# A transformer layer of two cross-attention blocks in one loop: the same operations issued in another order

## The chip, the cores and the metric

The kernel runs on one core of one Trainium2 chip. The metric is the device time of one execution in microseconds. A core has five engines that each take their own instructions in order: TensorE (PE in the profile; PEld is its weight load), VectorE (DVE), ScalarE (ACT), GpSimd (POOL) and SyncE (SP), which here only issues DMAs. They meet at semaphores.

## The reference

64 samples of 128 rows by 320 columns, `x`, and a context of 128 rows by 192 columns, `ctx`, go through two blocks. The first attends from `x` to the first 124 rows of the context (8 heads), adds a second result from the last four context rows ("tokens"), projects, and adds `x`. The second is a transformer layer: self attention (20 heads), cross attention to the context (20 heads), and a gated feed-forward, each after a layer norm and with a residual.

```python
query = hidden_states @ Wq; keyt = enc @ Wk; valt = enc @ Wv
hs = _mha(query, keyt, valt)
ca_hs1 = _mha(ca_q1, residual, residual)          # token queries attend to x
ca_hs2 = _mha(ca_hs1 @ Wq, ca @ Wk_ca, ca @ Wv_ca)
x = (hs + ca_hs2) @ Wout + b_out + residual
h1 = _ln(x, n1_g, n1_b)
x = _attn(h1, h1, q1, k1, v1, o1_w, o1_b, heads) + x
h2 = _ln(x, n2_g, n2_b)
x = _attn(h2, context, q2, k2, v2, o2_w, o2_b, heads) + x
h3 = _ln(x, n3_g, n3_b)
a, g = jnp.split(h3 @ ff_w1 + ff_b1, 2, axis=-1)
ff = a * jax.nn.gelu(g, approximate=False) @ ff_w2 + ff_b2
return ff + x
```

## The kernel before

Two samples make a step (`G = 2`, 32 steps). The loop runs 33 passes, and one pass holds work of several steps at once: the first block of step i, self attention and cross attention of the step before it, and the feed-forward of the one before that. A head that computes factors and loads weights stands ahead of the loop, and a last feed-forward behind it.

The order of the work is written out by hand. `BODY` names the "jobs" of a pass, the results that PE writes to six PSUM banks in turn (`J_BANKS`); each engine's own program then calls its part of every job in its own order. A job may start when the reader of the job six places ahead has released the bank (`bank_free`). Names used below:

- `XTj_b`: transpose of the normalised rows of block b for layer j. ScalarE writes the high half precision part of it to `hTn` (`high_blocks`), VectorE the low part (`low_blocks`).
- `K1T0..2`, `Q1T0..2`: chunks of self keys and queries from `hTn`. ScalarE writes the high part (`high_shifted`), VectorE the whole value (`whole_shifted`), GpSimd the difference (`low_split`). `Q0Tk`, `K0Tk` (first block), `K2Tk` (cross keys): chunks whose low part VectorE writes (`low_chunk`). SP writes the chunks to scratch memory in DRAM (`put`, L360) and reads them back stacked by head as `Qs`, `Ks`, `Q0s`, `K0s` (`stack`, L364).
- `S0..S27`: scores of a unit of four heads; VectorE takes the row maxima (`maxima`, L896). `mx0..mx7`: those maxima transposed, into `mxs`.
- `T0..T27`: the same scores the other way round, less the maxima. ScalarE writes two exponentials of each, `P` and `PT` (`exps`, L649 and L650), and GpSimd their difference (`low_probabilities`, L462). `attend(n)` then multiplies `PT` with the values (V0, VX, V1, V2). Units 0 to 3 are the token queries, 4 to 13 self, 14 to 23 cross, 24 to 27 the first block.
- `outTj_b`, `outMj_b`: transpose and projection of the attention output, then `residual`, `deviation` (GpSimd) and `norm`. `ff0..ff9`, `y0`, `y1`: feed-forward. `kca`, `vca`, `M4`, `caT`, `s4`, `p4T`, `hs`: the tokens' path. `G`: the token gains for the next pass.

SP's queue matters too. `load_step(i + 1, i)` issues the nine loads of the next step (`xT`, `cT`, `ca32`, `xin`, and `cT2`, this step's context once more, for the cross keys and values that the next pass uses), each of which adds 16 to `step_loaded`. It stands behind the stacks of the first block and behind a wait for the low part of `V0_1`, the last reader of `cT`:

```python
                sp.wait_ge(v_done, v_job(i, LOOP_JOBS, "V0_1"))
                sp.wait_ge(xa_ready, i * G + G)
                sp.wait_ge(ca_ready, i + 1)
                sp.wait_ge(vx_ready, i * G + G)
                load_step(i + 1, i)
```

## Time and profile before

| | |
|---|---|
| median of 3 runs | 4520.15 us (4511.48 to 4526.72) |
| the profiled execution | 4524.91 us |
| its span | 4523.1 us |
| PE busy | 3916.9 us, 87% |
| DVE, ACT, POOL busy | 57%, 50%, 44% |
| TensorE clock granted, mean | 0.90 of full speed |
| bytes moved by DMA | 232.60 MB, 51 GB/s |

A row of a timeline gives the start in us from the span's start, the duration, the engine, the source line, the operation, what is written and read, how many instructions the row merges, and in square brackets the idle time before it with what ended it. TensorE's clock has two levels, 2.4 GHz (1.0) and 1.2 GHz (0.5); a granted clock between them is the mean of a stretch. In the list of waits a row says who waited at which line for whose result, the total, the count and the longest.

### The profile page before, as it was taken

The numbers are of one execution on the slowest core, as the hardware profiler recorded it, in microseconds if no ns is written. First come the engines' busy times: TensorE is split into PE (matmuls) and PEld (weight loads), VectorE is DVE, ScalarE is ACT, GpSimd is POOL, SyncE is SP. The second block draws the span as 40 slices with busy tenths as digits, with TensorE's granted clock in tenths as the row PEclk, the third lists the DMA queues.
The fourth block names the chain that finished last, engine by engine and source line by source line (L and its number), as shares of the span: only waits on it lengthen the run. The fifth ranks groups of instructions, "written<-read, shape, count | busy, mean of one in ns | idle before, by whom it ended". The sixth has DMA issues, their size and how long they took to land.

```text
span 4523.1 us, 114162 instructions
## 1 busy us (share of the span) xinstructions
PE 3916.9 (87%) x39220; PEld 3138.1 (69%) x39220; DVE 2589.3 (57%) x6409; ACT 2246.6 (50%) x3834; POOL 1978.1 (44%) x2297
## 2 busy tenths in 40 slices
...
GB/s 125 55 53 48 35 51 45 56 58 52 54 35 51 46 56 58 51 54 32 47 52 56 58 49 57 32 47 52 56 58 49 57 32 47 52 56 57 49 47 28
DMA packets 394133, 232.60 MB, mean 51 GB/s; under 512 B 24806, under 2 KB 393054, under 8 KB 393182
## 3 DMA queue, kind: packets, MB, share of 16 engines
...
## 4 chain that ended last, share of the span: by engine, by line
PE 34%; issue 30%; POOL 24%; DVE 7%; ACT 2%; DMA 2%; POOLq 1%; DVEq 0%; SPq 0%; ACTq 0%
PE bank L1291 31%; POOL PT L462 11%; POOL ca_heads L495 3%; PE bank L1332 2%; POOL cK L469 1%; POOL cQ L469 1%; DMA out<-X 1%; POOL XA L455 1%; POOL VX L484 1%; DVE OB L944 1%; POOL VX L483 1%; DVE OB L966 1%; POOL OA L482 1%; ACT P L631 1%; POOL XB L455 1%
## 5 line engine op out<-in xcount | busy, mean ns | idle before, releaser
L462 POOL TENSOR_TENSOR PT<-P,PT 128x512 f16<-128x512 f32 (+1 forms) x924 | 1066.8, 1155 | 1073.5 <-ACT PT L650 1073.5
L896 DVE TENSOR_REDUCE mx<-bank 128x4 f32<-128x512 f32 (+1 forms) x924 | 598.8, 680 | 236.9 <-PE bank L1291 232.1
L1291 PE MATMUL bank<-hT,w_ff_w 128*128 128x256 f16 x5440 | 645.7, 275 | 0.8 <-DVE hT L925 0.8
L1291 PE MATMUL bank<-mxs,pick 84*128 84x128 f16 (+1 forms) x3696 | 613.0, 242 | 0.0
L1291 PEld LDWEIGHTS bank<-hT,w_ff_w 128*128 128x128 f16 x5440 | 539.0, 100 | 73.1 <-DVE hT L925 1.2
L1291 PE MATMUL bank<-V,PT 128*128 128x17 f16 (+1 forms) x9504 | 371.3, 175 | 117.9 <-POOL PT L462 114.0
L1291 PEld LDWEIGHTS bank<-V,PT 128*128 128x128 f16 (+1 forms) x9504 | 334.0, 100 | 177.1 <-POOL PT L462 163.6
L1291 PE MATMUL bank<-Qs,Ks 96*128 96x128 f16 x2640 | 452.3, 248 | 2.4
L1291 PEld LDWEIGHTS bank<-mxs,pick 84*128 84x128 f16 (+1 forms) x3696 | 418.7, 115 | 26.1 <-issue 11.3
L631 ACT ACTIVATE P<-bank,ff_b,scale 128x256 f32<-128x256 f32 x340 | 191.6, 564 | 411.6 <-PE bank L1291 336.3
L1291 PE MATMUL bank<-w_ff,F 128*128 128x320 f32 x1360 | 389.9, 434 | 1.3 <-DVE F L972 1.3
L502 POOL TENSOR_TENSOR rstd<-mv,eps 128x1 f32<-128x1 f32 x198 | 41.1, 208 | 659.6 <-DVE mv L960 658.3
L972 DVE SCALAR_TENSOR_TENSOR F<-bank,ff_b,P 128x256 f32<-128x256 f32 x340 | 163.8, 482 | 280.7 <-ACT P L631 279.7
L1291 PE MATMUL bank<-hTn,w_k 128*128 128x256 f16 (+1 forms) x792 | 160.6, 387 | 180.5 <-DVE hTn L925 180.5
L1291 PEld LDWEIGHTS bank<-Qs,Ks 96*128 96x128 f16 x2640 | 298.9, 114 | 19.4 <-DVE mxs L905 5.4
L1291 PEld LDWEIGHTS bank<-w_ff,F 128*128 128x128 f32 x1360 | 248.9, 190 | 89.7 <-DVE F L972 1.5
L649 ACT ACTIVATE P<-bank,log_p,out_factor 128x512 f32<-128x512 f32 x330 | 256.1, 776 | 51.1 <-PE bank L1291 31.7
L790 DVE TENSOR_SCALAR whole<-bank,factor,qk_b 128x256 f32<-128x256 f32 (+1 forms) x297 | 157.0, 538 | 205.4 <-ACT cK L581 145.2
L649 ACT ACTIVATE P<-bank,log_p,exp_self 128x512 f32<-128x512 f32 x330 | 256.8, 778 | 27.5 <-PE bank L1291 24.9
L1291 PEld LDWEIGHTS bank<-hTn,w_k 128*128 128x128 f16 (+1 forms) x792 | 105.9, 141 | 233.9 <-DVE hTn L925 188.3
L650 ACT ACTIVATE PT<-bank,log_p,exp_self 128x512 f16<-128x512 f32 x330 | 256.6, 777 | 0.0
L650 ACT ACTIVATE PT<-bank,log_p,out_factor 128x512 f16<-128x512 f32 x330 | 253.8, 769 | 0.0
...
## 6 DMA issues: line engine op xcount, KB each, us to landing
...
xin<-in_x SPq DMA_DIRECT2D x34, 320.0 KB, 3.4
```

What stands on the lines that cost most here:

```text
L455: nc.gpsimd.tensor_tensor(dst[:, b, :], src[:, b, :], bias[:, j, :], ALU.add).then_inc(ready, 1)
L462: nc.gpsimd.tensor_tensor(PT[0:keys, n % PT_SLOTS, 1, :], P[0:keys, n % P_SLOTS, :], PT[0:keys, n % PT_SLOTS, 0, :], ALU.subtract).then_in ...
L469: nc.gpsimd.tensor_tensor(dst[0:r, 1, k, :], whole[0:r, m % 3, :], dst[0:r, 0, k, :], ALU.subtract)\
L495: nc.gpsimd.tensor_tensor(ca_heads[:, :, :], ca16[:, :].unsqueeze(1).to_broadcast([rows, HEADS0, GS]), mask_ca[:, :].unsqueeze(2).to_broad ...
L631: nc.scalar.activation(gate[:, t % 2, :], bank[:, 0:GS], ACT.Gelu, scale=scale[:, 1:2], bias=ff_b[:, FFT + t:FFT + t + 1]).then_inc(a_done, 1)
L649: nc.scalar.activation(P[0:keys, n % P_SLOTS, :], bank[0:keys, :], ACT.Exp, bias=log_p[0:keys, :], scale=by)
L650: nc.scalar.activation(PT[0:keys, n % PT_SLOTS, 0, :], bank[0:keys, :], ACT.Exp, bias=log_p[0:keys, :], scale=by).then_inc(a_done, 1)
L790: nc.vector.tensor_scalar(whole[0:r, m % 3, :], bank[0:r, 0:GS], factor[0:r, FQ2:FQ2 + 1], qk_b[0:r, c + k:c + k + 1], ALU.mult, ALU.add). ...
L896: nc.vector.tensor_reduce(mx[:, g % 2, 4 * u:4 * u + 4], bank[:, :].rearrange("p (h s) -> p h s", h=4)[:, :, 0:keys], axis=AX.X, op=ALU.ma ...
L972: nc.vector.scalar_tensor_tensor(out=F[:, t, :], in0=bank[:, GS:2 * GS], scalar=ff_b[:, t:t + 1], in1=gate[:, t % 2, :], op0=ALU.add, op1= ...
L1291: return nc.tensor.matmul(o, lhsT, rhs, start=start, stop=stop)
L1332: last = nc.tensor.transpose(bank[0:r, k * S:(k + 1) * S], src[:, b, at[k]:at[k] + r], ident[:, :])
```

## The change

`BODY`, and with it the programs of PE, ACT and DVE, are put in another order; the operations stay. In short:

- A pass begins with XT0_0, the first queries Q0T0 and Q0T1, the token scores S0 and S1, XT0_1, Q0T2, S2, S3, and only then K1T. Before, the two transposes came first and K1T directly behind them.
- The value product of unit n stands behind the exponents of unit n + 2 (before: n + 1).
- K0T0, K0T1 and the transposes caT stand ahead of S4. K2T0 and K2T1 move from behind the feed-forward to between the self exponents, with a wait for `step_loaded` ahead of K2T0; K2T2 and the V2 products move in among the cross exponents; the products of y0 and y1 are cut into more pieces and moved forward.
- VectorE's `turn_factors` runs at the end of a pass for the next, not at its start.
- SP writes Q0T first, on semaphores of its own (`q0_put`, `k0_put` for `first_put`), and `load_step` issues the two `cT2` loads first.
- The column of ones of V0 and V2 is written once per block.

```diff
 BODY = jobs_of("""
-    XT0_0 XT0_1 K1T0 K1T1 K1T2 Q1T0 Q1T1 Q1T2
+    XT0_0 Q0T0 Q0T1 S0 S1 XT0_1 Q0T2 S2 S3 K1T0 mx0 K1T1 K1T2 Q1T0 mx1 Q1T1 Q1T2
...
             def load_step(i, before):
+                for k, r in enumerate(CHC):
+                    sp.dma_start(cT2[0:r, k, :], d["cT"][before, k * r:(k + 1) * r, :]).then_inc(step_loaded, 16)
                 for k, r in enumerate(CH0):
...
             def one_pass(i, stores):
+                put_lows(i, "Q0T", cQ, CH0, s_q0, AT0, q0_put)
                 put_splits(i, "K1T", cK, s_k1, self_put)
...
-                put_lows(i, "Q0T", cQ, CH0, s_q0, AT0, first_put, self_stacked)
-                put_lows(i, "K0T", cK, CH0, s_k0, AT0, first_put)
+                put_lows(i, "K0T", cK, CH0, s_k0, AT0, k0_put, self_stacked)
                 sp.wait_ge(j_full, done(i - 1, LOOP_JOBS.number("T27"), "J"))
-                sp.wait_ge(first_put, i * STACK_STORES + STACK_STORES)
+                sp.wait_ge(q0_put, i * CROSS_STORES + CROSS_STORES)
                 stack(Q0s, s_q0, D0, Q_PARTS, first_stacked)
+                sp.wait_ge(k0_put, i * CROSS_STORES + CROSS_STORES)
                 stack(K0s, s_k0, D0, K_PARTS, first_stacked)
...
             def turn_factors(i):
-                dve.wait_ge(next_ready, i + 1)
+                dve.wait_ge(next_ready, i + 2)
...
+                pe.wait_ge(step_loaded, i * LOADS_STEP + 2 * LOADS_STEP)
+                chunk(i, "K2T", 0, "k2", CHC, cT2, AT1, CH1)
+                attend(i, 7)
                 exponents(i, 9)
-                attend(i, 7)
+                chunk(i, "K2T", 1, "k2", CHC, cT2, AT1, CH1)
+                attend(i, 8)
                 exponents(i, 10)
-                attend(i, 8)
+                attend(i, 9)
...
                 ff(i, L, 0)
                 attend(i, 12)
+                ff(i, L, 1)
                 attend(i, 13)
-                ff(i, L, 1)
+                ff(i, L, 2)
                 turn_out(i, 1, 1)
...
-                bank = j_ahead(i, "y0", 2)
-                v_job_done(i, L, "ff8")
-                ff_products(bank, 0, 0, 6)
+                bank = j_ahead(i, "y0", 5)
+                v_job_done(i, L, "ff7")
+                ff_products(bank, 0, 0, 5)
                 scores(i, 14)
                 scores(i, 15)
```

First place: PE at the start of a pass. In the kernel before, the two transposes of XT0 (`OA`) and then the chunks of K1T (`w_k`):

```order
L1298 ISA
L1332 MATMUL bank<-ident,OA 128x128 x3
L1501 REGISTER_ALU
L1298 REGISTER_ALU
L1332 MATMUL bank<-ident,OA 128x128 x3
L1336 ISA
L1298 REGISTER_ALU
L1291 MATMUL bank<-hTn,w_k 128x256 x8
```

And in the changed kernel, where `w_Wq` is a chunk of Q0T and `G,ca_heads` a unit of token scores:

```order
L1342 MATMUL bank<-ident,OA 128x128 x3
L1308 REGISTER_ALU
L1301 MATMUL bank<-xT,w_Wq 120x256 x3
L1308 REGISTER_ALU
L1301 MATMUL bank<-xT,w_Wq 120x256 x3
L1430 REGISTER_ALU
L1346 REGISTER_ALU
L1301 MATMUL bank<-G,ca_heads 128x128 x4
L1308 REGISTER_ALU
L1301 MATMUL bank<-G,ca_heads 128x128 x4
L1511 REGISTER_ALU
L1308 REGISTER_ALU
```

The second transpose comes behind two query chunks and two units of scores; one more chunk and two more units follow it ahead of `w_k`.

Second place: DVE at the start of a pass. Before, behind the loop's branch, the factors (L880 to L888) and the low parts of XT0 (`hTn`):

```order
L1154 ISA
L880 COPY out_factor<-factor 128x2
L772 ISA
L881 COPY out_factor<-next_factor 128x1
L882 COPY factor<-next_factor 128x12
L772 REGISTER_ALU
L883 TENSOR_SCALAR out_inverse<-out_factor 128x3
L772 REGISTER_ALU
L886 TENSOR_SCALAR out_inverse<-out_inverse,scale 128x3
```

Now, with `cQ` the low part of a query chunk and `mx` the maxima of a unit:

```order
L1164 ISA
L930 SCALAR_TENSOR_TENSOR hTn<-bank,hTn 128x2x128
L933 SCALAR_TENSOR_TENSOR hTn<-bank,hTn 64x128
L787 REGISTER_ALU
L803 SCALAR_TENSOR_TENSOR cQ<-bank,factor,cQ 120x256
L787 REGISTER_ALU
L803 SCALAR_TENSOR_TENSOR cQ<-bank,factor,cQ 120x256
L789 ISA
L904 TENSOR_REDUCE mx<-bank 128x4
```

The factors are gone from here; two query chunks and two units of maxima stand between the low parts of XT0_0 and XT0_1.

Third place: PE in the self attention of the changed kernel, behind T8 (`Qs,Ks` and `mxs,pick`); the ISA row at L1656 is the new wait for `step_loaded`, and `cT,w_k` is K2T0:

```order
L1301 MATMUL bank<-Qs,Ks 128x128
L1301 MATMUL bank<-mxs,pick 128x128
L1656 ISA
L1308 REGISTER_ALU
L1301 MATMUL bank<-cT,w_k 128x256 x2
L1478 REGISTER_ALU
L1301 MATMUL bank<-V,PT 128x17 x12
L1346 REGISTER_ALU
```

In the kernel before this chunk stands behind the feed-forward, with no wait for the loads of its own ahead of it.

## Rows read from the trace of the kernel before

**Rows 1.** The page, part 1: busy time, share and instructions of each engine.
```profile
PE 3916.9 (87%) x39220; PEld 3138.1 (69%) x39220; DVE 2589.3 (57%) x6409; ACT 2246.6 (50%) x3834; POOL 1978.1 (44%) x2297
```
**Rows 2.** The waits of PE: engine, line, waited for, total, times, longest.
```profile
PE bank L1291 <- DVE hTn L925: 186.7, 66, 5.9
PE bank L1291 <- POOL PT L462: 151.0, 232, 1.5
...
PE bank L1332 <- DVE OB L944: 70.8, 99, 1.3
...
PE bank L1291 <- DMA Qs<-scratch_q: 7.3, 17, 0.6
```
**Rows 3.** Line L1519, once a pass: duration, first and last start.
```profile
L1519 PE MATMUL bank<-ident,p x33: 272/273/273, 179.4 to 4424.3; 128*128 128x128 f32 x33
```
**Rows 4.** Windows of one pass: length, busy PE, PEld, DVE, ACT, POOL, clock, DMA share, GB/s.
```profile
2360.90:2379.90 19.00, 13.03 (x68) 8.69 (x67) 12.19 (x36) 4.12 (x9) 4.89 (x8) 0.91 0.05 15
2379.90:2402.10 22.20, 19.84 (x203) 15.40 (x204) 10.19 (x28) 10.81 (x19) 9.85 (x12) 0.92 0.53 76
2402.10:2427.00 24.90, 22.50 (x279) 18.33 (x280) 16.32 (x36) 17.68 (x31) 11.31 (x11) 0.95 0.44 111
2427.00:2463.00 36.00, 33.72 (x287) 27.41 (x286) 22.03 (x56) 12.17 (x21) 15.89 (x22) 0.99 0.27 45
2463.00:2490.80 27.80, 23.89 (x346) 20.55 (x345) 14.91 (x35) 22.43 (x36) 17.62 (x18) 0.82 0.03 10
```
**Rows 5.** Timeline of PE around the start of that pass and at S4.
```profile
2373.34 0.87 PE L1332 MATMUL bank<-ident,OA 128*128 128x128 f32 x6
2379.88 4.58 PE L1291 MATMUL bank<-hTn,w_k 128*128 128x256 f16 x24 [5.67 <-DVE hTn L925]
2384.40 2.91 PE L1291 MATMUL bank<-hTn,w_q 128*128 128x256 f16 x24
...
2402.07 0.62 PE L1291 MATMUL bank<-Ks,Qs 96*128 96x128 f16 x8 [0.37 <-DMA Qs<-scratch_q]
```
**Rows 6.** Timeline of DVE: last residual, first instruction behind the branch, token maxima.
```profile
2368.62 0.55 DVE L955 SCALAR_TENSOR_TENSOR XA<-bank,out_inverse,XA 128x320 f32<-128x320 f32 x1 [1.54 <-PE bank L1291]
...
2376.96 0.36 DVE L880 COPY out_factor<-factor 128x2 f32<-128x2 f32 x1 [2.46 <-issue]
...
2388.49 1.27 DVE L896 TENSOR_REDUCE mx<-bank 128x4 f32<-128x512 f32 x2
```
**Rows 7.** Timeline of POOL: the last split of Q1T.
```profile
2388.65 0.66 POOL L469 TENSOR_TENSOR cQ<-whole,cQ 64x256 f16<-64x256 f32 x1 [0.31 <-DVE whole L790]
```
**Rows 8.** Timeline of DVE: the low part of V0_1.
```profile
2419.90 0.54 DVE L809 SCALAR_TENSOR_TENSOR V<-bank,factor,V 128x320 f16<-128x320 f32 x1
```
**Rows 9.** Timeline of SP's queue: first and last loads of a step, stack of cross queries.
```profile
2420.89 1.38 SPq L351 DMA_DIRECT2D xT<-in_xT  x3
...
2424.44 0.82 SPq L357 DMA_DIRECT2D cT<-in_cT  x2
...
2449.54 1.34 SPq L364 DMA_DIRECT2D Qs<-scratch_q  x3
```
**Rows 10.** The DMA view: issues, KB each, median us to landing.
```profile
xin<-in_x SPq DMA_DIRECT2D x34, 320.0 KB, 3.4
```
**Rows 11.** Timeline of ACT in the cross units: P of units 15, 16, 19 and 20.
```profile
2465.20 0.78 ACT L649 ACTIVATE P<-bank,log_p,out_factor 128x512 f32<-128x512 f32 x1
...
2466.57 0.78 ACT L649 ACTIVATE P<-bank,log_p,out_factor 128x512 f32<-128x512 f32 x1
...
2471.02 0.78 ACT L649 ACTIVATE P<-bank,log_p,out_factor 128x512 f32<-128x512 f32 x1 [0.20 <-PE bank L1291]
...
2472.61 0.78 ACT L649 ACTIVATE P<-bank,log_p,out_factor 128x512 f32<-128x512 f32 x1
```
**Rows 12.** The page, part 5: group of L462, GpSimd's difference.
```profile
L462 POOL TENSOR_TENSOR PT<-P,PT 128x512 f16<-128x512 f32 (+1 forms) x924 | 1066.8, 1155 | 1073.5 <-ACT PT L650 1073.5
```
**Rows 13.** Line L357, the loads of cT2: time to landing.
```profile
DMA to landing us min/median/max: 2.8/4.4/8.5
```
**Rows 14.** Timeline of PE: the transpose behind Q2T, and S14 with S15.
```profile
2445.46 0.33 PE L1530 MATMUL bank<-ident,ext_wide 128*128 128x128 f32 x1
...
2456.30 0.61 PE L1291 MATMUL bank<-Ks,Qs 96*128 96x128 f16 x8
```

More of the change, by code:

```diff
@@ L109 @@
 BODY = jobs_of("""
[L110 to L118 removed]
+    XT0_0 Q0T0 Q0T1 S0 S1 XT0_1 Q0T2 S2 S3 K1T0 mx0 K1T1 K1T2 Q1T0 mx1 Q1T1 Q1T2
+    T0 V1_0 T1 kca T2 V1_1 T3 vca M4 K0T0 K0T1 caT0 caT1
+    S4 S5 S6 K0T2 S7 S8 V0_0 mx2 S9 S10
+    T4 S11 T5 S12 V0_1 T6 S13 s4 T7 mx3 T8 K2T0 T9 K2T1 T10 T11 outT1_0 T12 outM1_0 T13
+    ff0 ff1 ff2 outT1_1 ff3 outM1_1 ff4 p4T ff5 XT1_0 XT1_1 ff6 Q2T0 Q2T1 Q2T2 mT ff7 mB ff8 ff9
+    S14 S15 S16 S17 S18 y0 mx4 S19 S20
+    T14 S21 T15 K2T2 T16 S22 T17 S23 T18 mx5 T19 S24 T20 S25 T21 mx6 T22 outT2_0 T23 S26 V2_0
+    T24 outM2_0 T25 S27 mx7 V2_1 T26 outT2_1 T27 outM2_1 hs0 outT0_0 hs1 y1 outM0_0 outT0_1 XT2_0 XT2_1 outM0_1 G
 """)
@@ L355, in load_step @@
                 sp.dma_start(xin[:, :, :], d["x"][i, :, :, :].rearrange("g s c -> s g c")).then_inc(step_loaded, 16)
-                for k, r in enumerate(CHC):
-                    sp.dma_start(cT2[0:r, k, :], d["cT"][before, k * r:(k + 1) * r, :]).then_inc(step_loaded, 16)
             def put(src, k, r, dst, at, landed):
@@ L1149, in _ @@
             link(-1, nc.vector.tensor_scalar(exp_self[:, :], exp_self[:, :], D1 ** -0.5, None, ALU.mult))
[L1150 removed]
+            for b in range(G):
+                ones_column(V1, b, HEADS1, D1, out_factor[:, 1:2])
+            turn_factors(-1)
             low_tokens(-1, HEAD_JOBS)
@@ L1694, in _ @@
                 scores(i, 20)
-                chunk(i, "K2T", 1, "k2", CHC, cT2, AT1, CH1)
                 exponents(i, 14)
```

363 lines of the change are left out of this document (182 added, 181 removed).

## The prediction

> **What bounds the kernel now.** I read the page's busy line first: PE is busy for 87% of the span and no other engine for over 57% [rows 1]. So the time is PE's work, at the clock that it is granted, plus PE's idle time. The list of waits, kept to PE, says what ends that idle time: 187 us for `hTn` from DVE, 151 us for `PT` from POOL, 71 us for `OB` from DVE, 7 us for a DMA of Qs [rows 2]. One transpose that occurs once a pass starts at 179.4 us and, 32 passes later, at 4424.3 us [rows 3]: a pass takes 132.6 us, and there are 33.
>
> I then took one pass apart in five stretches by the windows view [rows 4], with these marks: end of the value product of unit 27; start of the first key chunk K1T0; start of S4, the first self scores; start of ff0; start of T14, the first cross exponents; end of unit 27 again. They last 19.0, 22.2, 24.9, 36.0 and 27.8 us: 129.9 us, a quick pass. The clock column matters as much: 0.82 in the fifth stretch, 0.91 and 0.92 in the first two. The mean pass is 2.7 us longer than this one, with the same instructions; I put that down to more half clock in some passes.
>
> **The change, stretch by stretch.** No instruction's shape changes but that the column of ones is now written per block (some 0.3 us of DVE a pass, beside other work). What is priced is where waits fall.
>
> *Stretch 1, unit 27 to K1T0: 19.0 becomes about 18.0 us.* Before, PE ends its two transposes and idles 5.67 us until K1T0 [rows 5]. The DVE rows show why: after the token gains (`G`) DVE stands 2.46 us at the loop's branch, ended by "issue", and only then come the factors (1.3 us) and the low parts of XT0 (1.5 us), which take it to K1T0 [rows 6]. The change puts Q0T (three chunks, some 1.35 us each) and S0 to S3 (0.9 us) in that hole, and the factors ahead of the branch. But the hole is DVE's chain, not a lack of PE work, and the chain gets other links. After the change it runs: last residual with its statistics 1.35, factors 1.3, norm 0.45, tokens 0.5, branch 2.46, low XT0_0 0.75, two low query chunks 0.95, two maxima 1.27 (the pair of [rows 6]), low XT0_1 0.7: 9.7 us. Against that, the old chain from the residual's start at 2368.62 to K1T0 at 2379.88 is 11.3 us [rows 5, 6]. The last residual itself starts later, since low parts and norms of the block before now stand ahead of it on DVE: 8.3 us behind unit 27 instead of 7.7. Sum 18.0. PE idles still, in three pieces of 2.1, 2.3 and 1.3 us, because Q0T2 reuses the bank that the low part of XT0_0 must release.
>
> *Stretch 2, K1T0 to S4: 22.2 becomes 20.6 us.* S4 starts when the stacked queries have landed; PE waited 0.37 us for that DMA [rows 5]. The chain is: K and Q chunks on PE, last split on POOL, ending at 2389.31 [rows 7], then puts and stacks until 2402.07, which is 12.8 us. At full clock, with the two maxima's transposes put in, the chunks take 5.9 us (24 matmuls 2.9 us; the K group took 4.58, mostly at half clock [rows 5]). Then 1.9 to the last split, and 12.8. PE's own work there: 19.8 us busy [rows 4], less 1.7 for K's half clock, 1.4 and 0.9 for Q0T0 and S0 to S3, and 2.6 more for K0T and two transposes, some 18.4 us. So it waits about 2 us for the DMA, a wait that takes the place of the old one and hides as much half clock in the slow passes.
>
> *Stretch 3, S4 to ff0: 24.9 becomes 27.7 us, the dear one.* PE now waits for `step_loaded` ahead of K2T0, and the count is that of all nine loads of the next step. SP can issue them only when the low part of V0_1 is done: it ended at 2420.44, and the first load was issued at 2420.89 [rows 8, 9]. The nine issues take 4.4 us and the `xin` load lands 3.4 us after its issue [rows 9, 10]. That cT2 is now issued first helps nothing. V0_1's low part comes 9.6 us behind S4 (it was 18.4): 5.1 us to T4 (five maxima at 0.65 and what is between), two units of ScalarE at 1.37 us [rows 11], two copies. So the loads are complete at 9.6 + 0.45 + 4.4 + 3.4 = 17.8 us. PE comes to K2T0 at 12.0 us (two more units on ScalarE, then POOL's 1.155 us [rows 12]) and stands 5.8 us. Behind it in PE's queue are all of units 7 to 13, so ScalarE and POOL run dry too. Then five units, two chunks, one projection: 9.9 us. Bounds: no stall if the loads are earlier than I think (22.3 us), and 31 us if the last load lands 3 us later, which is within the range of landings of the cT2 loads [rows 13].
>
> *Stretch 4, ff0 to T14: 36.0 becomes 34.1 us.* Out go K2T0 and K2T1 (about 0.9 us each, now in stretch 3), and one of the waits for `OB` shrinks by some 0.5 us, since ff1 and ff2 stand ahead of the transpose. But one ff block less, and one product of y0 less, stand between Q2T and S14. Q2T ended as the transpose behind it began, at 2445.46; the stacked queries were issued from 2449.54, and S14 started at 2456.30 without a wait [rows 9, 14]. So they land at most 10.8 us behind Q2T; I take 10.3. PE gets there after 7.3: a new wait of 3 us. 19.3 + 10.3 + 4.5 = 34.1.
>
> *Stretch 5, T14 to unit 27: 27.8 becomes 25.7 us.* This is where the value products lag. ScalarE paces it: a unit each 1.37 us, 1.59 us where PE is at half clock [rows 11]. The lag takes away PE's waits for `PT`, but those are the shadow of ScalarE's pace: 14 x 1.36 + 3.3 for the copies that now lie inside (two of V2, K2T2, two of hTn, three maxima) = 22.3, and 3.4 for the first exponent, POOL, and what PE has queued before unit 27.
>
> Sum at full clock: 18.0 + 20.6 + 27.7 + 34.1 + 25.7 = 126.1 us against 129.9.
>
> **The clock** takes most of that back. The old pass went to half clock after its 5.67 us of idleness (K group 4.58 instead of 2.9 us) [rows 5], and in the light work of stretch 5, at 0.82 [rows 4]. The new one has idle pieces of 5.7 us together ahead of K1T0, 2.5 ahead of S4, 5.8 ahead of K2T0, 3 ahead of S14. I add 1.7 for K1T, 1.2 for K2T and its neighbours, 1.0 for stretch 5: 3.9, so a pass of 130.0, and 130.3 with what slow passes still lose. Bounds: 0 and 8 us.
> The Trainium skill, page "TensorE: Matmul & The Clock Gate", section "HAM oscillation — how this bites in real kernels", says that a DMA wait in front of each short burst of matmuls throttles the engine each time, so that every burst starts cold; by it the three DMA waits of the new pass would each be paid for twice. The K group here agrees for one idle stretch; no row shows it yet for a DMA wait.
>
> Mean pass 132.6 to 130.3: 2.3 us x 33 = 76 us. Head and tail do not change but for one factors chain (1.3 us). The profiled execution took 4524.9 us; less 76 is 4449. It stood 5 us above the median of 4520, so I say **4445**.
>
> **Rivals.**
> - *The K2T stall is not there, or short* (the loads are early enough, or PE is late). For: the sum brings PE to K2T0 with no clock loss on the way, and a PE that comes late waits less. Then stretch 3 is 22.3 to 24, a pass 125 to 127: 4270 to 4340. Against: the nine loads follow V0_1 strictly [rows 8, 9], and they move with it. Chance 0.22.
> - *Slower, by the K2T stall*: one wait at `step_loaded`, 9 us rather than 5.8, with ScalarE and POOL empty behind it. It decides from about 8 us: 2.3 us of net gain are used up. At 9 us a pass is 133.5, so 4555. For: it stands in PE's in-order queue in the middle of a stage paced by ScalarE. Chance 0.15.
> - *Slower, by the clock*: each new wait is followed by a half-clock stretch as K1T's is, and the units between T9 and ff0, light work as in stretch 5, stay there too. 4 us more than I added: 134.3 a pass, 4580. This is the rule cited above. Chance 0.08.
> - *No difference*: gains and stalls cancel, 4507 to 4534. Chance 0.08.
> - *The forecast's case*, 4340 to 4505: 0.47.
>
> **Numbers.** Faster 0.22 + 0.47 = 0.69, same 0.08, slower 0.23. "Same" is within 0.3%, about what a measurement of this kernel can tell. The range is 4290 to 4565: it leaves out some 0.08 below and 0.10 above.
>
> **What would show it.** In PE's waits, `hTn` from DVE falls from 187 to below 120 us, but does not vanish; `PT` falls below 60; a wait for a DMA of `xin` or `cT` appears at the first K2T chunk, near 190 us in all; waits for Qs grow from 7 to over 100 us. The DVE keeps its 2.4 us at the branch. If the wait at K2T0 is below 2 us a pass, the third stretch is wrong and the time is near 4300; if S4 does not wait for its DMA, stretch 1 or PE's load is mis-sized; if K1T runs at full clock and the total clock rises above 0.93, the clock term is.

## The result, and the profile after

The changed kernel took 5074.9 us (median of 4 runs, 5068.3 to 5077.5) against 4523.2 us for the kernel before (4 runs): a ratio of 1.122, 95% interval 1.120 to 1.125. It is 12% slower. The forecast was 4445 us, 1.7% faster, with a range to 4565: wrong in sign and far outside the range. The ratios of the experiments below are each against the kernel before as timed in the same round (medians 4514.8 to 4531.4 us).

The page's busy line of the changed kernel answers to [rows 1], and the list of waits, PE only (who waited at which line, for whom: us in total, times, longest), to [rows 2]:

```profile
PE 4233.4 (84%) x39220; PEld 3361.7 (66%) x39220; DVE 2543.2 (50%) x6482; ACT 2246.4 (44%) x3834; POOL 1977.4 (39%) x2297
```
```profile
PE bank L1301 <- DMA Qs<-scratch_q: 148.8, 64, 3.4
PE bank L1301 <- DVE hTn L933: 123.8, 105, 1.7
PE bank L1301 <- DMA xin<-in_x: 110.8, 33, 5.1
PE bank L1301 <- DVE mxs L913: 78.0, 99, 1.5
PE bank L1301 <- POOL PT L463: 77.7, 142, 1.0
PE bank L1342 <- DVE OB L952: 53.4, 33, 2.0
PE bank L1342 <- issue: 49.3, 32, 1.9
PE bank L1301 <- issue: 48.7, 32, 1.7
```

PE's busy time grew by 316 us with the same matmuls, which is 9.6 us a pass; its idle time grew by 227 us, 6.9 a pass. So the waits alone do not tell the story: the larger part is that the same matmuls took longer. The windows view of one pass, with the marks of [rows 4], shows where it went (columns: window, length, busy PE, PEld, DVE, ACT, POOL with counts, granted clock, DMA share, GB/s):

```profile
2341.17:2362.69 21.52, 17.19 (x92) 12.22 (x87) 13.74 (x38) 4.57 (x10) 4.86 (x8) 0.84 0.08 22
2362.69:2383.95 21.26, 17.96 (x197) 14.73 (x195) 11.34 (x34) 11.06 (x21) 10.26 (x12) 1.00 0.57 82
2383.95:2418.89 34.94, 30.21 (x262) 24.49 (x263) 13.01 (x30) 16.05 (x27) 10.37 (x9) 0.52 0.27 72
2418.89:2454.94 36.05, 32.22 (x280) 25.82 (x279) 20.59 (x54) 13.03 (x22) 16.43 (x22) 0.99 0.25 38
2454.94:2491.19 36.25, 29.62 (x359) 23.46 (x360) 15.49 (x37) 22.58 (x36) 17.63 (x18) 0.81 0.05 15
```

Read the third row first: S4 to ff0 ran at a clock of 0.52, half clock almost without a break, and took 34.9 us instead of 24.9 [rows 4]. The fifth, T14 to unit 27, took 36.3 instead of 27.8 us at about the old clock. Those two hold the loss. The second stretch had full clock (0.92 before).

For the experiments I use means over the passes of one traced execution (29 passes, worked out from PE's rows and the recorded clock). The mark at the end of unit 27 is the start of the PE instruction behind its value product; in e7 PE stands idle for a microsecond there, and the mark is the product's end. Each cell is length in us, then half-clock time.

| kernel, median us | unit 27 to K1T0 | to S4 | to ff0 | to T14 | to unit 27 | pass |
|---|---|---|---|---|---|---|
| before, 4523 | 19.1 / 2.8 | 23.6 / 7.0 | 25.4 / 4.3 | 36.0 / 0.7 | 28.2 / 11.5 | 132.3 / 26.3 |
| after, 5075 | 20.8 / 5.4 | 21.1 / 0.1 | 35.0 / 32.3 | 36.1 / 0.5 | 36.3 / 14.0 | 149.2 / 52.2 |
| e1, 5015 | 20.7 / 5.4 | 23.2 / 0 | 31.6 / 18.7 | 34.8 / 0.9 | 37.5 / 17.8 | 147.7 / 42.7 |
| e16, 4929 | 20.4 / 4.8 | 21.1 / 0 | 30.6 / 10.2 | 35.1 / 1.5 | 37.8 / 18.7 | 145.1 / 35.2 |
| e3, 4933 | 21.0 / 5.9 | 21.0 / 0.1 | 30.7 / 27.2 | 36.0 / 0.8 | 36.5 / 14.0 | 145.1 / 48.0 |
| e5, 4825 | 21.0 / 5.7 | 21.1 / 0.1 | 28.4 / 25.9 | 36.0 / 0.8 | 36.3 / 13.7 | 142.8 / 46.1 |
| e6, 4752 | 20.8 / 5.2 | 21.2 / 0 | 23.0 / 9.9 | 37.8 / 1.9 | 36.7 / 15.5 | 139.5 / 32.4 |
| e2, 4901 | 21.8 / 3.1 | 21.0 / 0.2 | 34.4 / 28.6 | 38.2 / 3.4 | 28.4 / 13.2 | 143.7 / 48.4 |
| e4, 4773 | 17.0 / 4.5 | 24.1 / 8.5 | 25.5 / 5.0 | 36.8 / 0.7 | 36.7 / 15.4 | 140.0 / 34.0 |
| e7, 4990 | 23.1 / 8.1 | 27.8 / 17.5 | 25.7 / 5.1 | 36.4 / 0 | 33.8 / 20.5 | 146.8 / 51.2 |
| e9, 4568 | 16.6 / 2.5 | 23.7 / 7.2 | 25.2 / 3.2 | 36.0 / 0.8 | 32.4 / 12.0 | 133.9 / 25.6 |
| e14, 4653 | 19.1 / 2.1 | 25.1 / 10.8 | 25.2 / 3.8 | 35.9 / 0.5 | 31.1 / 16.8 | 136.5 / 34.0 |
| e15, 4654 | 19.1 / 2.1 | 25.1 / 10.8 | 25.2 / 3.6 | 35.9 / 0.6 | 31.1 / 17.1 | 136.5 / 34.1 |
| e11, 4574 | 19.1 / 2.5 | 25.4 / 11.7 | 25.4 / 4.3 | 35.8 / 0.3 | 27.9 / 6.3 | 133.6 / 24.9 |
| e8, 4679 | 21.6 / 2.2 | 24.5 / 10.2 | 25.4 / 4.8 | 36.6 / 0.7 | 29.1 / 14.0 | 137.2 / 31.9 |
| e12, 4554 | 19.2 / 1.3 | 24.1 / 9.1 | 25.1 / 4.1 | 35.8 / 0.2 | 29.2 / 14.2 | 133.4 / 29.0 |
| e10, 4576 | 22.1 / 3.3 | 21.1 / 0 | 23.0 / 9.9 | 39.3 / 4.3 | 28.4 / 12.1 | 133.9 / 29.7 |
| e13, 4505 | 21.8 / 2.6 | 21.1 / 0 | 23.0 / 9.9 | 36.9 / 1.4 | 28.8 / 13.0 | 131.6 / 26.9 |
| e17, 4430 | 19.1 / 3.5 | 22.1 / 3.4 | 24.9 / 2.7 | 36.0 / 0.7 | 27.6 / 10.2 | 129.7 / 20.5 |
| e18, 4457 | 19.6 / 2.4 | 20.8 / 0.4 | 24.9 / 4.1 | 36.8 / 1.2 | 29.1 / 13.9 | 131.1 / 21.8 |

A mean can hide two kinds of passes. In the kernel before, 11 of the 29 passes take 135.0 to 135.1 us, with 11.6 us of half clock between K1T0 and S4; the other 18 take 129.8 to 131.2, with 4.3 us of it. So a cell such as 23.6 / 7.0 is a mixture of 25.3 / 11.6 and 22.6 / 4.3, and what an edit changes there can be how often each kind comes.

### The profile page after: what moved, and what is told of

Read it like the earlier page. It is cut to its first block, busy times and chain, and to the rows that moved or that the text cites. A ratio compares the mean times of both kernels' runs of the same rounds, so it can differ in the third digit from the quotient of the medians.

```text
span 5066.5 us, 114336 instructions
## 1 busy us (share of the span) xinstructions
PE 4233.4 (84%) x39220; PEld 3361.7 (66%) x39220; DVE 2543.2 (50%) x6482; ACT 2246.4 (44%) x3834; POOL 1977.4 (39%) x2297
## 4 chain that ended last, share of the span: by engine, by line
PE 41%; issue 17%; POOL 13%; DVE 11%; DMA 9%; ACT 5%; SPq 4%; POOLq 0%; DVEq 0%; ACTq 0%
PE bank L1301 38%; DMA Qs<-scratch_q 5%; POOL PT L463 2%; POOL ca_heads L496 2%; DMA xin<-in_x 2%; ACT PT L651 2%; DMA scratch_q<-cQ 2%; PE bank L1342 1%; SPq L364 1%; POOL cQ L470 1%; POOL cK L470 1%; POOL VX L485 1%; POOL VX L484 1%; DVE OA L974 1%; POOL OA L483 1%
## 5 line engine op out<-in xcount | busy, mean ns | idle before, releaser
L1301 PE MATMUL bank<-mxs,pick 84*128 84x128 f16 (+1 forms) x3696 | 714.9, 270 | 0.0
L1301 PE MATMUL bank<-Qs,Ks 96*128 96x128 f16 x2640 | 533.1, 278 | 78.0 <-DVE mxs L913 78.0
L1301 PEld LDWEIGHTS bank<-V,PT 128*128 128x128 f16 (+1 forms) x9504 | 380.3, 104 | 213.3 <-POOL PT L463 112.0
L1301 PEld LDWEIGHTS bank<-mxs,pick 84*128 84x128 f16 (+1 forms) x3696 | 464.2, 128 | 6.7
L1301 PE MATMUL bank<-w_ff,F 128*128 128x320 f32 x1360 | 423.3, 447 | 45.1 <-DVE F L980 45.1
L1301 PE MATMUL bank<-V,PT 128*128 128x17 f16 (+1 forms) x9504 | 384.3, 177 | 77.7 <-POOL PT L463 77.7
L1301 PE MATMUL bank<-Ks,Qs 96*128 96x128 f16 x2640 | 266.6, 249 | 148.8 <-DMA Qs<-scratch_q 148.8
L1301 PEld LDWEIGHTS bank<-Ks,Qs 96*128 96x128 f16 x2640 | 210.2, 114 | 212.0 <-issue 200.7
L503 POOL TENSOR_TENSOR rstd<-mv,eps 128x1 f32<-128x1 f32 x198 | 37.5, 189 | 692.1 <-DVE mv L968 691.7
L589 ACT ACTIVATE cK<-bank,factor 120x256 f16<-120x256 f32 (+2 forms) x198 | 93.4, 472 | 433.8 <-PE bank L1301 433.8
L607 ACT ACTIVATE hTn<-bank,out_factor 128x384 f16<-128x384 f32 x198 | 114.7, 580 | 373.2 <-PE bank L1342 373.2
L803 DVE SCALAR_TENSOR_TENSOR cK<-bank,factor,cK 120x256 f16<-120x256 f32 (+2 forms) x198 | 95.5, 482 | 355.8 <-ACT cK L589 355.6
```

The source lines that it names most:

```text
L589: nc.scalar.activation(dst[0:r, 0, k, :], bank[0:r, 0:GS], ACT.Copy, scale=factor[0:r, f:f + 1]).then_inc(a_done, 1)
L607: nc.scalar.activation(dst[:, 0:3, b * S:(b + 1) * S], bank[:, 0:3 * S].rearrange("p (k s) -> p k s", k=3), ACT.Copy, scale=scaled).then_i ...
L803: nc.vector.scalar_tensor_tensor(out=dst[0:r, 1, k, :], in0=bank[0:r, 0:GS], scalar=factor[0:r, f:f + 1], in1=dst[0:r, 0, k, :], op0=ALU.m ...
L1301: return nc.tensor.matmul(o, lhsT, rhs, start=start, stop=stop)
```

## The stage from S4 to ff0

PE's timeline of that pass: S4 behind its DMA wait, the last matmul of T8, and K2T0 behind the wait for the step's loads. K2T0's four matmuls take 2.07 us at half clock; a chunk of four such matmuls took 1.08 us in the kernel before at full clock.

```profile
2383.95 0.84 PE L1301 MATMUL bank<-Ks,Qs 96*128 96x128 f16 x12 [3.30 <-DMA Qs<-scratch_q]
...
2401.65 0.31 PE L1301 MATMUL bank<-mxs,pick 84*128 84x128 f16 x1
2405.07 2.07 PE L1301 MATMUL bank<-cT,w_k 96*128 96x256 f32 x4 [3.11 <-DMA xin<-in_x]
```

**e1.** Is the clock a consequence of the wait at S4? Fillers, matmuls whose result nobody reads, keep PE busy through it.

```diff
+            def warm(n):
+                for _ in range(n):
+                    mm(o_bank[1][:, 384:512], ident[:, :], ident[:, :])
...
+                warm(24)
                 scores(i, 4)
```

> The changed kernel (5074.9 us) with 24 idle matmuls (identity by identity, 128 columns each, some 2.7 us at full clock, into columns of an output bank that nobody reads) just ahead of S4, where PE waits 3.1 us a pass for the stacked queries. Theory 'clock': the wait drops PE to half clock and the light work behind it never brings it back, so with PE kept busy the stretch S4 to ff0 runs at full clock for most of its length and falls from 35.0 to about 30 us; 33 passes give 4910 us, half-clock time a pass from 52 to about 30 us. Rival 'light work': the work behind S4 is too thin for full clock whatever comes before it, or is paced by ScalarE and GpSimd: stretch 34 to 35.5 us, total 5050 to 5100.

Measured: 5015.1 us, ratio 1.109. The changed kernel goes to half clock within 2 us of S4 in 25 of 29 passes; with the fillers it never does before 10 us, and T8 came 12.6 us behind S4 instead of 16.8. Then the wait at K2T0 grew from 3.4 to 4.5 us a pass, since the loads had not moved as much. Half clock began 10.3 to 15.4 us behind S4, in most passes with T8, just ahead of that wait, and lasted nearly to ff0. The 24 fillers also took 5.4 us, 0.22 us each (twice what I had given them), and so held S4 up by 2 us. That the wait at S4 takes the clock of the next 10 us is shown; the total I expected forgot the second wait.

**e16.** Fillers in both waits.

```diff
+                warm(14)
                 scores(i, 4)
...
+                warm(16)
                 pe.wait_ge(step_loaded, i * LOADS_STEP + 2 * LOADS_STEP)
```

> The changed kernel (5074.9 us) with fillers in both DMA waits: 14 idle matmuls ahead of S4 and 16 (3.6 us at full clock) ahead of the wait for the step's loads at K2T0. With the first alone the stretch S4 to ff0 went from 35.0 to 31.6 us, at full clock up to T8, with a wait of 4.5 us at K2T0 and half clock behind it. Theory 'clock': with both filled, half clock from S4 to ff0 falls below 8 us and the stretch to 28 us; total 4860 to 4900. Rival 'light work': units T9 to T13 go to half clock by themselves: half clock stays above 14 us, the stretch above 30.5, total above 4950.

Measured: 4929.2 us, ratio 1.087. Half clock fell from 32.3 to 10.2 us, the stretch to 30.6. Between theory and rival: with both waits filled, 22 of the 32 us of half clock and 4.4 us of length are gone. What is left comes without a wait for a DMA: 5.9 us in the light end, around outT1_0, where the kernel before has its 4.3 us too, and 4.2 us between T7 and K2T0, in 22 of 29 passes.

**e3.** K2T0 and K2T1 back behind the feed-forward, and the wait with them.

```diff
                 exponents(i, 8)
-                pe.wait_ge(step_loaded, i * LOADS_STEP + 2 * LOADS_STEP)
-                chunk(i, "K2T", 0, "k2", CHC, cT2, AT1, CH1)
                 attend(i, 7)
                 exponents(i, 9)
-                chunk(i, "K2T", 1, "k2", CHC, cT2, AT1, CH1)
```

> The changed kernel with K2T0 and K2T1 back behind the feed-forward, and so without the wait for the step's loads among the self exponents. Theory 'K2T wait': 3.4 us of wait and 1.9 us of half-clock chunk leave the stretch S4 to ff0 (35.0 to 30), 1.8 us come into the next: a pass 3.5 us shorter, 4960 us. Rival 'shadow': the wait only takes the place of waits for GpSimd's PT, which come back (151 us of them before): 5040 or more. If the clock theory holds, half clock from S4 to ff0 stays in this run.

Measured: 4932.6 us, ratio 1.092. The stretch fell by 4.3 us and stayed at half clock for 27 of its 31 us, as the clock theory said. The rival, that waits for PT come back, holds too in part: PE's waits for PT rose from 77.7 to 141.8 us.

**e5.** While reading PE's order for this run I found that the description of the change above is wrong in one sentence. "The value product of unit n stands behind the exponents of unit n + 2 (before: n + 1)" is true of the token units 0 to 3 only. In the self units it is the reverse: before, `attend(4)` stood behind `exponents(6)`; now it stands ahead of it. In the units from 14 on it is n + 2 in both kernels.

```diff
                 exponents(i, 5)
                 scores(i, 12)
                 values(i, "V0", 1, "Wv", cT)
-                attend(i, 4)
                 exponents(i, 6)
+                attend(i, 4)
```
(and so on up to unit 11)

> The run with K2T0 and K2T1 put back (4932.6 us, 30.65 us from S4 to ff0, 27 us of it at half clock), and in addition the self units in the old relation of PE's queue: the value product of unit n behind the exponents of unit n+2, as the kernel before has it there, not n+1. Theory 'queue': with n+1 every exponents group stands in PE's queue behind a wait for GpSimd's PT, so ScalarE idles once a unit; put right, the stretch falls to about 27.5 us and the total to 4830. Rival 'clock alone': the order inside the stage does not matter, half clock sets its length: stretch 30 us or more, total 4915 or more.

Measured: 4825.0 us, ratio 1.065, 2.2 us off the stretch. In e3 PE waited 141.8 us for GpSimd's PT; with the old lag, 49.0 us (e3, then e5). So the change had made the self stage's lag worse, not better.

```profile
PE bank L1301 <- POOL PT L463: 141.8, 212, 1.5
```
```profile
PE bank L1301 <- POOL PT L463: 49.0, 138, 0.7
```

**e6.** The same with 14 fillers ahead of S4.

> As the run before it, with 14 idle matmuls (3.1 us at full clock) ahead of S4. Theory 'clock': with neither the idle time before S4 nor the load wait, the stage stays at full clock to its light end: half-clock time from S4 to ff0 under 10 us, stretch about 25.5 us, as in the kernel before; total 4770. Rival 'ScalarE's pace': without fillers the units are already paced by ScalarE and GpSimd, so full clock gives nothing: stretch within 0.7 us of the run without fillers and total within 25 us of it.

Measured: 4752.1 us, ratio 1.051. Half clock 25.9 to 9.9 us, the stretch 28.4 to 23.0 us, shorter than in the kernel before. The windows rows of the same stretch in e5 and then e6:

```profile
2423.60:2452.41 28.81, 27.11 (x253) 22.50 (x254) 12.32 (x28) 15.08 (x26) 10.39 (x9) 0.53 0.32 87
```
```profile
2376.33:2399.37 23.04, 19.44 (x254) 15.94 (x255) 12.56 (x28) 15.01 (x26) 10.40 (x9) 0.83 0.41 108
```

VectorE, ScalarE and GpSimd do the same work in both. PE does it with 8 us less busy time. 1.8 of the 5.4 us come back in the next stretch (36.0 to 37.8), where S14 now waits 1.1 us a pass for its DMA. The 12 us from 35.0 to 23.0 are now told apart, taken out in this order: 4.3 by K2T and its wait, 2.2 by the lag, 5.4 by the clock that the wait at S4 takes away. In another order the shares differ: fillers at S4 alone (e1) gave 3.4.

## The stage from T14 to unit 27

**e2 and e4.** The late order taken out of the changed kernel, and put into the one before. Both move everything behind S14 on PE, ScalarE and VectorE, and one `deviation` on GpSimd. They also move the pieces of y0 and the V2 products. The core, as e4 has it:

```diff
-                scores(i, 23)
                 exponents(i, 17)
+                scores(i, 23)
                 attend(i, 15)
-                turn_maxima(i, 5)
                 exponents(i, 18)
+                turn_maxima(i, 5)
                 attend(i, 16)
...
-                turn_out(i, 2, 0)
                 turn_maxima(i, 6)
...
                 exponents(i, 22)
+                turn_out(i, 2, 0)
```

> The changed kernel with everything behind S14 put back in the order of the kernel before (value products one unit behind, V2 and K2T2 at the end, y0 and y1 in the old pieces); K2T0 and K2T1 stay among the self exponents. Theory 'lag': the order of the cross and first-block units costs 8 us a pass, so T14 to unit 27 falls from 36.3 to about 28.5 us and the total to 4810. Rival 'state': that stretch is slow because of what comes before it (later stacks, half clock carried over), and stays above 34 us, total over 5000.

> The mirror of the run with the old late order: the kernel before (4523 us) with the changed kernel's order from S14 on, K2T0 and K2T1 where they were before, the column of ones per block. Theory 'lag': 8 us a pass are lost here too, 4790 us, and PE waits for mxs and for hTn at outM2. Rival 'state': with the old first half in front the new late order runs as forecast, 25.7 instead of 27.8 us: 4455 to 4523.

Measured: e2 4900.6 us (1.086), e4 4772.9 us (1.057). The stretch is 28.4 and 36.7 us: it follows its own order and nothing ahead of it. The pass moves by 5.5 and 7.7 us instead of 8, because other stretches give some back: in e2, ff0 to T14 takes 2.1 us more (S14 waits 2.2 us for its DMA instead of 1.3), and unit 27 to K1T0 1.0 more; in e4 unit 27 to K1T0 takes 2.1 us less, since K2T2 and the products of y1 now stand ahead of it.

What in that order costs? In the changed kernel PE waits twice as follows, and ScalarE stands still in between (PE's rows, then ScalarE's):

```profile
2461.52 0.46 PE L1301 MATMUL bank<-V,PT 128*128 128x17 f16 x12 [0.58 <-POOL PT L463]
2463.45 0.23 PE L1301 MATMUL bank<-Qs,Ks 96*128 96x128 f16 x1 [1.48 <-DVE mxs L913]
```
```profile
2462.17 0.77 ACT L651 ACTIVATE PT<-bank,log_p,out_factor 128x512 f16<-128x512 f32 x1
2462.83 0.25 ACT L621 ACTIVATE mxs<-bank 20x128 f16<-20x128 f32 x1
2464.21 0.78 ACT L650 ACTIVATE P<-bank,log_p,out_factor 128x512 f32<-128x512 f32 x1 [1.13 <-POOL PT L463]
```

T19 needs the maxima of its group, ScalarE copies them only after the exponentials of unit 18, and it has no exponent to work on until T19 is done. A third wait stands at outM2_1, 6 us ahead of the end of unit 27; the late stage of the kernel before has none for `hTn`, and every run with the new late order has it, 1.6 us a pass:

```profile
2484.94 1.26 PE L1301 MATMUL bank<-w_o_w,hTn 128*128 128x320 f16 x8 [1.65 <-DVE hTn L933]
```

**e14 and e15.** Single moves in the kernel before.

```diff
-                turn_maxima(i, 5)
                 exponents(i, 18)
+                turn_maxima(i, 5)
```

> The kernel before with one move of the change alone: mx5, the transposed maxima of the second cross group, behind T18 instead of ahead of it, on PE and ScalarE. Theory 'bubble': ScalarE's copy of mx5 and VectorE's low part now stand between the exponents of units 18 and 19, PE waits 1.4 us for mxs ahead of T19 and ScalarE runs dry: T14 to unit 27 grows from 28.2 to 29.8 us, total 4575. Rival: PE has slack there and nothing is measured, 4510 to 4535.

```diff
+                turn_maxima(i, 6)
+                exponents(i, 22)
                 turn_out(i, 2, 0)
-                turn_maxima(i, 6)
                 scores(i, 26)
-                exponents(i, 22)
...
+                low_maxima(i, 6)
                 normalise(i, 4)
                 low_out(i, 2, 0)
-                low_maxima(i, 6)
```

> The kernel before with another move alone: outT2_0 behind T22, and VectorE's low part of mx6 ahead of the normalisation that outT2_0 waits for. Theory: PE's wait for OB grows from 0.4 to 1.6 us and everything behind it with it: T14 to unit 27 from 28.2 to 29.5 us, total 4565. Rival: the wait takes the place of others, 4510 to 4535.

Measured: 4653.1 us (ratio 1.026) and 4653.6 us (1.027). PE's waits for mxs in the kernel before, then the waits of e14, then of e15:

```profile
PE bank L1291 <- DVE mxs L905: 23.1, 33, 0.9
```

```profile
PE bank L1291 <- DVE mxs L905: 78.9, 66, 1.6
PE bank L1332 <- DVE OB L944: 66.8, 99, 1.3
```
```profile
PE bank L1332 <- DVE OB L944: 109.4, 99, 1.6
PE bank L1291 <- DVE mxs L905: 29.9, 33, 0.9
```

Each is the wait foreseen: mxs 23.1 to 78.9 us, OB 70.8 [rows 2] to 109.4. They add 1.7 and 1.2 us a pass, and the traced passes of both grow by 4.2, over twice what I gave them. With that goes 5.3 to 5.6 us more half clock in the stage, and 3.8 more from K1T0 to S4, where nothing was touched. Two waits of unlike length have one price, and the passes show why: in both runs they alternate, but for one pass of e14. 14 of 29 take 137.6 to 137.7 us, with 17.4 us of half clock between K1T0 and S4; all but one of the others take 135.4 to 135.7, with 4.2 us there and 20 us in the late stage. So the edit does not add its wait to a pass, it sets which kinds of passes the loop goes through. No run fills these waits, so that the rest is the clock alone is not shown.

**e7 and e9.** The other two corners of a square. "Order of groups" stands here for all of the new late order but K2T2 and y1: also the pieces of y0 and the places of the V2 products. PE work moved: K2T2 and the products of y1 (4.5 us at full clock) behind or ahead of unit 27.

```diff
                 attend(i, 26)
+                bank = j_ahead(i, "y1", 4)
+                ff_products(bank, 1, 0, 4)
                 attend4(i, 0)
                 values(i, "V2", 1, "v2", cT2)
+                ff_products(bank, 1, 4, 6)
                 attend(i, 27)
```
(e9, with K2T2 behind `exponents(i, 15)`; e7 is e4 with both undone)

> The kernel before with the new late order (4772.9 us), but the products of y1 and the chunk K2T2, 4.5 us of PE work, back behind unit 27. Theory 'cover': they were cover for VectorE's chain behind unit 27, and ahead of it they only delay that chain: T14 to unit 27 falls from 36.7 to 32.5 us, unit 27 to K1T0 grows from 17.0 to about 19.2; total 4705. Rival 'order of the groups': PE is idle enough there that 4.5 us of work cost nothing, and the loss is all in the new places of the transposed maxima and of outT2_0: stretch above 35.5 us, total 4760 to 4840.

> The fourth corner of a square: the kernel before with the order of its groups untouched, but K2T2 among the cross exponents and the products of y1 ahead of unit 27, 4.5 us of PE work moved into the late stage. The other corners: neither 4526, order and work 4773, order alone 4990. Theory 'group order': the loss is the new order of groups (transposed maxima one unit ahead of their exponents, outT2_0 later); moved work by itself keeps PE busier and its clock higher, T14 to unit 27 grows from 28.2 to 31 us, unit 27 to K1T0 falls from 19.1 to 17, total 4530 to 4580. Rival 'work': moved work is what lengthens the stage, in full: stretch above 33 us, total above 4640.

| | old order of groups | new order of groups |
|---|---|---|
| work behind unit 27 | before, 132.3 us, half clock 26.3 | e7, 146.8, half clock 51.2 |
| work ahead of it | e9, 133.9, half clock 25.6 | e4, 140.0, half clock 34.0 |

Measured: e9 4568.3 us (1.010), e7 4990.2 us (1.103). Both of my theories for e7 fell. Taking 4.5 us of work out of the stage shortened it by only 2.9 us, and made the pass 6.8 us longer: with the new order of groups the stage was at half clock for 20.5 us, and there was half clock at the pass's start (8.1 us) and in the token stage (17.5 us), in every pass. In the old order the same work costs 4.2 us in the stage, nearly in full, although PE idles for 3.9 us there, and gives 2.5 back ahead of K1T0. So of the stage's 8 us the moved work is about half. Of the pass it is 1.6 us, and the order of groups 6.1 (e4 against e9) to 14.5 (e7 against before); the two differ mostly in the stretches up to S4, where e7 has far more half clock.

## Fillers in the kernel before, and parts joined

**e8, e12, e11.** Fillers in the kernel before, in e8, then (10 in place of 22) in e12; and in e11.

```diff
+                warm(22)
                 v_job_done(i, L, "XT0_1")
```
```diff
+                warm(6)
                 attend(i, 14)
```

> The kernel before (4515 us in the last comparison) with 22 idle matmuls (4.9 us at full clock) in PE's 5.6 us of idle time ahead of K1T0, and nothing else changed. Theory 'clock': K1T's three chunks take 2.9 instead of 4.76 us and the half clock behind them (7 us a pass up to S4) mostly goes: a pass 2 to 3 us shorter, 4435 us, which would beat both kernels. Rival 'chain': what stands behind K1T waits for VectorE, GpSimd and the stacks, the gain becomes idle time before S4, and that brings half clock back later: 4495 to 4530.

> The kernel before with only 10 idle matmuls ahead of K1T0 instead of 22 (4678.6 us, where the fillers started 2.2 us late with an idle time that nothing but issue ended, and so overshot by 2.5 us). Theory 'overshoot': 10 of them fit, K1T0 starts where it did, the K group takes 2.9 us instead of 4.76: 4440 to 4500 if the token stage behind keeps its clock as before. Rival 'half clock moves': a K group at full clock lets the token stage fall to half clock in nearly every pass, as with 22 (10.2 instead of 7.0 us before S4): a gain of 1.9 and a loss of 1.5 us a pass, 4500 to 4550.

> The kernel before with 6 idle matmuls (1.3 us at full clock) in PE's 1.55 us wait ahead of the value product of unit 14, the wait that comes 1.8 us before half clock begins. Theory 'clock': half clock there starts later or not at all: half-clock time from T14 to unit 27 from 11.5 to under 6 us, stretch 28.2 to 26.5, total 4470. Rival 'light work': one wait filled does not matter: half clock above 10 us, total 4500 to 4550.

Measured: 4678.6 us (1.034), 4554.1 (1.008), 4573.6 (1.014): all slower than the kernel before, and e8 and e11 slower than either theory had them. PE's rows in e8 show why 22 are too many: 2.41 us of the 5.67 us of [rows 5] are now idle time by "issue", which nothing released; the fillers start behind it and take 6.7 us instead of 4.9, partly at half clock.

```profile
2304.57 0.87 PE L1336 MATMUL bank<-ident,OA 128*128 128x128 f32 x6
2307.84 6.70 PE L1291 MATMUL bank<-ident 128*128 128x128 f32 x44 [2.41 <-issue]
2314.38 2.90 PE L1291 MATMUL bank<-hTn,w_k 128*128 128x256 f16 x24
```

The K group did take 2.9 instead of 4.8 us. But in all three the untouched token stage had more half clock (10.2, 9.1 and 11.7 us for 7.0). e11 halved half clock behind T14, gained only 0.3 us there, and lost 1.8 us ahead of S4. Why so little was gained is not shown.

**e17 and e18.** PE has two short waits in the token stage, 0.87 us for mx and 1.12 us for PT.

```diff
+                warm(3)
                 turn_maxima(i, 0)
...
+                warm(4)
                 attend(i, 0)
```

> The kernel before with 3 idle matmuls ahead of mx0 (PE waits 0.87 us there) and 4 ahead of the first value product (1.12 us), nothing else. Theory 'short waits': half clock between K1T0 and S4 falls from 7.0 us a pass to the 4 of the K group, S4 waits for its DMA instead and the stretch falls only from 23.6 to 23.1: total 4500 to 4520. Rival 'thin work': the clock falls in the token stage in spite of the fillers, half clock stays at 7 us or more: 4520 to 4560.

> The same with 10 idle matmuls ahead of K1T0 as well (alone these gave 4554 us: the K group 1.8 us faster, 9.1 us of half clock in the token stage). Theory 'short waits': full clock from K1T0 to S4, half clock there under 2 us; the stretch is then set by the stacks and falls from 23.6 to 21.5 us, and the total to 4450 to 4470, faster than every kernel so far. Rival 'thin work': as above, half clock stays above 7 us and the total above 4520.

Measured: e17 4429.7 us, ratio 0.980 (0.978 to 0.983); e18 4456.8, 0.986 (0.983 to 0.989). The theory of short waits holds for the clock, and e17 gained 90 us where I had given it 20 at most: S4 came 1.5 us sooner, and the stages behind it had 3 us less half clock and were 1.1 us shorter. K1T0 to S4 in two passes of the kernel before, then in two of e17:

```profile
2113.72:2138.99 25.27, 23.28 (x202) 18.38 (x203) 10.04 (x27) 10.54 (x19) 10.24 (x12) 0.77 0.46 66
2248.88:2271.83 22.95, 20.45 (x202) 15.73 (x202) 10.31 (x28) 10.80 (x19) 9.96 (x12) 0.89 0.52 73
```
```profile
2197.29:2219.28 21.99, 21.43 (x216) 17.04 (x217) 10.04 (x27) 10.80 (x19) 9.68 (x12) 0.92 0.53 76
2326.96:2348.99 22.03, 21.45 (x217) 17.04 (x217) 10.05 (x28) 10.80 (x19) 9.71 (x12) 0.92 0.53 76
```

The kernel before has its two kinds of passes, 130 to 131 us and 135 us; all 29 of e17 take 129.6 to 129.8, with 3.3 to 3.5 us of half clock ahead of S4. That is the difference between quick and mean pass which the prediction put down to half clock in some passes: it was so. In e18 the stretch to S4 is shorter still (20.8 us), but the two from ff0 on are 0.8 and 0.9 us longer than in the kernel before, as in e8, and e18 stays behind e17.

**e10 and e13.** Parts that were better joined: new pass start, 14 fillers ahead of S4, K2T0 and K2T1 and the late stage as before, self units with n + 2; in e13 also the old feed-forward order.

```diff
 BODY, e13 against e10
-    ff0 ff1 ff2 outT1_1 ff3 outM1_1 ff4 p4T ff5 XT1_0 XT1_1 ff6 Q2T0 Q2T1 Q2T2 mT ff7 mB ff8 ff9
+    ff0 ff1 outT1_1 ff2 outM1_1 ff3 p4T ff4 XT1_0 XT1_1 ff5 Q2T0 Q2T1 Q2T2 mT ff6 mB ff7 ff8 ff9
```

> Parts that were better joined: the new start of a pass, the 14 idle matmuls ahead of S4, K2T0 and K2T1 behind the feed-forward, self units with n+2, and the whole late stage as before. If stretches add: unit 27 to K1T0 21.0, to S4 21.1, to ff0 23.0, to S14 30.5, to T14 6.7, to unit 27 28.4: 130.7 us a pass against 132.2, so 4475 us, faster than both. Rival 'the clock does not add': a stage that is unchanged in order goes to half clock at another place, as K1T's token stage did when the idle time before it was filled: 4600 or more.

> The combination (4575.7 us) with the feed-forward stage in the old order too, ff0 to ff9 with outT1_1, outM1_1 and Q2T one block earlier. Theory 'one block later': ff0 to S14 was 31.1 us there against 29.3, since the transposed queries start one block later and S14 then waits for its DMA, with 3.3 us of half clock behind it; put back, ff0 to T14 falls from 39.4 to 36.5 us, total 4480, faster than the kernel before. Rival 'chain': ff0 now comes 2.3 us earlier against VectorE's and ScalarE's work, so the wait for OB stays whatever the order: 4550 to 4590.

Measured: e10 4575.7 us (1.012), e13 4504.7 us, ratio 0.995 (0.993 to 0.996). e10 came out nearer to its rival: ff0 to T14 took 39.3 us, with 4.3 at half clock. In e13 it took 36.9, so the old feed-forward order is worth 2.4. e13 is 0.5% faster than the kernel before of its own round and missed its forecast of 4480; e17 is the fastest of all.

## Why the prediction was wrong, by its own steps

- **Stretch 5 (25.7; measured 36.3) is the largest miss, 10.6 us.** Three premises failed. "This is where the value products lag" misread the order; there the lag is the same in both kernels. "ScalarE paces it", so PE's work is free: 4.5 us moved in cost 4.2 (e9). And I priced exponents alone, not what stands between the groups: mx5 and outT2_0 each add a wait, and each lengthens this stretch by 2.9 us alone (e14, e15). In e4, where all moves stand together, work and order make 8.5 us, so these do not add up one by one; the wait for `hTn` at outM2_1 (1.6 us) was never taken out alone, and its share stays open.
- **Stretch 3 (27.7; 35.0) was rightly called the dear one, and mis-sized.** PE came to K2T0 18.0 us behind S4 (forecast 12.0), the loads were there at 21.1 (forecast 17.8): a stall of 3.1 in this pass, not 5.8. The first load left at 2396.97, behind the low part of V0_1:

```profile
2395.97 0.55 DVE L818 SCALAR_TENSOR_TENSOR V<-bank,factor,V 128x320 f16<-128x320 f32 x1
```
```profile
2396.97 0.86 SPq L351 DMA_DIRECT2D cT<-in_cT  x2
...
2400.96 1.35 SPq L357 DMA_DIRECT2D xin<-in_x  x1
```
  The chain was the predicted one, 3 us later. The units around the stall, priced at full clock, ran at half. Experiments put 5.4 us on the clock lost at S4, 4.3 on K2T, 2.2 on the shorter lag, which the description of the change had the wrong way round.
- **The clock term (3.9, bounds 0 and 8) was too small, and its upper bound too.** I charged half clock to the groups directly behind each wait. Half-clock time a pass went from 26.3 to 52.2 us, and PE's busy time with the same matmuls grew by 9.6 us a pass. The other part of the miss is waiting, which grew by 6.9 us a pass. The rival "slower, by the clock" named the place ("the units between T9 and ff0"), got 0.08, and was itself too mild: 134.3 a pass. (The times of the two slower rivals, 4555 and 4580, leave out the 5 us that the forecast takes off; with them they are 4550 and 4577.) At S4 the rule cited there (the Trainium skill, "TensorE: Matmul & The Clock Gate", "HAM oscillation — how this bites in real kernels": a DMA wait ahead of short bursts makes each start cold) agrees with the trace: half clock within 2 us of S4 in 25 of 29 passes, in none with fillers (e1, e16). At K2T0 the clock was down already. The rule does not show at S14, where the transposed queries were also late, by 1.3 us, and the stretch kept 0.99; there feed-forward products stand on both sides, but that they are the reason was not tested. Nor has it to be a DMA: filling waits for mx and PT of about 1 us took half clock away in the token stage (e17).
- **Stretch 1 (18.0; 20.8).** VectorE's chain was right: the last residual starts 8.7 us behind unit 27 (forecast 8.3), the low part of XT0_0 5.4 behind it (6.1), with 1.62 us at the branch for 2.46:

```profile
2349.89 0.54 DVE L963 SCALAR_TENSOR_TENSOR XA<-bank,out_inverse,XA 128x320 f32<-128x320 f32 x1
...
2355.32 0.42 DVE L930 SCALAR_TENSOR_TENSOR hTn<-bank,hTn 128x256 f16<-128x256 f32 x1 [1.62 <-issue]
```
  But PE has a stop of its own at the start of a pass:

```profile
2351.99 0.54 PE L1342 MATMUL bank<-ident,OA 128*128 128x128 f32 x3 [1.39 <-issue]
2352.37 1.03 PE L1301 MATMUL bank<-xT,w_Wq 120*120 120x256 f32 x4
2355.14 3.77 PE L1301 MATMUL bank<-xT,w_Wq 80*120 80x256 f32 x8 [1.74 <-issue]
```
  These 3.1 us stand in place of part of the old wait, and half clock follows (5.4 us). From the low part to K1T0 it took 7.4 us, not 3.7.
- **Stretch 2 (20.6; 21.1) and stretch 4 (34.1; 36.1).** Right in mechanism: a DMA wait at S4 of 3.1 us (2), at S14 of 1.3 (3). The feed-forward's y0 and Q2T got 1.3 and 0.9 us of waits that I had not seen. K1T ran at full clock, so its 1.7 us of clock term were not needed.
- **The signs given.** Only Qs came out as said, 149 us (over 100). `hTn` fell from 187 to 124 us (below 120 foreseen), PT from 151 to 78 (below 60), `xin` came to 111 us (190), VectorE's stop at the branch to 1.62 us (2.4). All moved the way foreseen, and none of them told 149 us a pass from 130; the granted clock did, with 0.83 for 0.90 in the whole execution.
